# A graph network on one core: the SBUF map of two stages redrawn

## The reference

```python
# L0: sparse weight matrix built from the edges
x = _layernorm(x + (x @ W.T + bias))
# L1: RMS norm, 1024 -> 256, graph attention with 4 heads (softmax over the incoming edges), 256 -> 1024
x = _layernorm(x + _L1(x, edge_index, rms_w, W_down, Wl, Wr, att, W_up))
# L2: graph convolution
x = _layernorm(x + relu(segment_sum((x @ W)[src] * norm, dst) + b))
# L3: two graph layers of the form  h @ W_self + mean(h[src]) @ W_neigh + b
x = _layernorm(x + _L3(x, src, dst, W_self0, W_neigh0, b0, W_self1, W_neigh1, b1))
```

## Time and profile before

| | us |
|---|---|
| median of three runs | 1559.93 |
| the profiled execution, first to last instruction | 1553.5 |
| TensorE busy | 1433.6 (92%) |
| VectorE busy | 783.6 (50%) |
| ScalarE busy | 421.9 (27%) |
| GpSimd busy | 254.4 (16%) |

### The profile page before, as it was taken

The page is one execution under the profiler, slowest core; times in us unless marked ns, Lnnn a source line. Parts: engine busy times, 40 slices in busy tenths (PEclk is TensorE's granted clock), DMA queues, the critical chain, the costliest instruction groups (busy, mean ns, idle before and its releaser), DMA issues.

```text
span 1553.5 us, 17781 instructions
## 1 busy us (share of the span) xinstructions
PE 1433.6 (92%) x6845; PEld 1145.2 (74%) x6845; DVE 783.6 (50%) x1359; ACT 421.9 (27%) x716; POOL 254.4 (16%) x309
## 2 busy tenths in 40 slices
PE   3988999748999989899999999999999999999996
PEld 3876888625666656678888888888888888888884
DVE  6996776517888868754336632221033232411243
ACT  7853222235565545312111100110120001201000
POOL 3000000064666655110000010000000100000000
PEclk9997999969999999999999999999999999999998
DMA  1665344454555644152117552230056544400252
GB/s 46 192 181 189 106 126 116 93 157 150 163 155 153 179 146 130 55 185 85 61 42 240 180 189 85 103 145 1 0 190 219 187 124 147 143 1 0 91 194 95
DMA packets 101988, 195.95 MB, mean 126 GB/s; under 512 B 26856, under 2 KB 61465, under 8 KB 101905
## 3 DMA queue, kind: packets, MB, share of 16 engines
q1 hardware_dynamic: 77434, 121.01, 25.8%
q0 software_dynamic: 22800, 73.61, 13.9%
q10 hardware_dynamic: 1670, 0.21, 0.1%
HBM read 140.86 MB, written 53.92 MB: 125 GB/s over the span
## 4 chain that ended last, share of the span: by engine, by line
PE 56%; DVE 1%; DMA 0%; issue 0%; POOL 0%; DVEq 0%; ACT 0%
PE layers_y_ps L1927 35%; PE layers_y_ps L1948 17%; PE layers_turn_ps L1911 2%; PE layers_up_ps L1894 1%; PE layers_y_ps L1964 1%; DMA x_d<-fetched_x 0%; DVE layers_w_lo L2082 0%; DVE layers_y L2126 0%; PE layers_y_ps L1972 0%; DVE layers_y L597 0%; DVE layers_ln_stats L591 0%; PE layers_turn_ps L1882 0%; DVE layers_parts_lo L2099 0%; DVEq L592 0%; PE layers_y_ps L1882 0%
## 5 line engine op out<-in xcount | busy, mean ns | idle before, releaser
L1948 PE MATMUL layers_y_ps<-layers_parts_hi,layers_counts 128*128 128x512 f32 x464 | 143.6, 391 | 0.0
L1948 PE MATMUL layers_y_ps<-layers_parts_lo,layers_counts 128*128 128x512 f32 x464 | 143.3, 390 | 0.0
L1927 PE MATMUL layers_y_ps<-layers_w_hi,layers_parts_hi 128*128 128x512 f32 x400 | 126.0, 396 | 0.0
L1927 PE MATMUL layers_y_ps<-layers_w_lo,layers_parts_hi 128*128 128x512 f32 x400 | 123.6, 390 | 0.0
L1927 PE MATMUL layers_y_ps<-layers_w_hi,layers_parts_lo 128*128 128x512 f32 x400 | 123.5, 390 | 0.0
L509 POOL DMA_INDIRECT attention_got<-xl_d,attention_src x104 | 106.5, 1024 | 63.1 <-DVE attention_weighted L1537 31.3
L1948 PEld LDWEIGHTS layers_y_ps<-layers_parts_lo,layers_counts 128*128 128x128 f32 x464 | 87.1, 188 | 18.7
L1948 PEld LDWEIGHTS layers_y_ps<-layers_parts_hi,layers_counts 128*128 128x128 f32 x464 | 86.9, 188 | 18.9
L1353 PE MATMUL attention_mix_ps<-attention_weighted,attention_hot 128*110 128x260 f32 x368 | 95.7, 384 | 3.7 <-DVE attention_weighted L1537 3.7
L1320 PE MATMUL attention_row_ps<-attention_bent,edges_att_rows 128*128 128x512 f32 x184 | 97.1, 611 | 0.0
L2099 DVE SCALAR_TENSOR_TENSOR layers_parts_lo<-layers_y_ps,layers_parts_hi 128x1024 fp32r<-128x1024 f32 x16 | 19.6, 1225 | 147.5 <-ACT layers_parts_hi L2043 147.5
(11 more groups left out here) (341 smaller groups left out, 2783.4 us busy)
## 6 DMA issues: line engine op xcount, KB each, us to landing
layers_counts<-counts_d SPq DMA_DIRECT2D x30, 640.0 KB, 4.0
layers_rest<-x_d SPq DMA_DIRECT2D x23, 512.0 KB, 4.1
self_d<-layers_y POOLq DMA_DIRECT2D x20, 512.0 KB, 6.0
x_d<-layers_y POOLq DMA_DIRECT2D x19, 512.0 KB, 2.9
fetched_x<-x_d SPq DMA_DIRECT2D x17, 512.0 KB, 3.7
fetched_raw<-in_L_gnn_W_self POOLq DMA_DIRECT2D x16, 512.0 KB, 5.9
fetched_raw<-in_L_gnn_W_neigh POOLq DMA_DIRECT2D x16, 512.0 KB, 9.0
heads_dst_wide<-in_dst_held SPq DMA_DIRECT2D x13, 512.0 KB, 4.0
```

The lines of the kernel that those rows point to most:

```text
L1927: last = nc.tensor.matmul(y_ps[n % 2][:, a:a + HALF], rows_in[t][:, k * P:(k + 1) * P], w[k][:, a:a + HALF], start=(k == 0 and p == 0), st ...
L1948: last = nc.tensor.matmul(y_ps[n % 2][:, a:a + HALF], counts[c % 2][:, k, :], part[k][:, a:a + HALF], start=(k == 0 and part is hi), stop= ...
```

## The change

No instruction is added, removed or moved. Only addresses change.

- `Memory.at` places a tile at a given address. The 10 tiles of weights and `up` parts of `Fetched` now lie at `base`, which is where the tiles held through the attention end (57.5 KiB). A tile named `split_weights` keeps that room free of other tiles in both stages.
- In attention the tiles from `xr` on are allocated behind that room, in a new order: `xr`, `hot_t`, `bent`, `score_rows`, then the small index tiles, `scaled`, `got`, `dst_wide1`, `far`, and the rest as before.
- In the layers `w_hi3` and `w_hi4` lie in front of the room, and behind it `parts_lo`, `counts`, `w_hi5` to `w_hi7`, `w_lo3` to `w_lo7`, `y`, `side`, `rest`, `mixed_hi` and `mixed_lo`.
- `raw`, `x` and `mixed` of `Fetched` move up to the top of SBUF.

The addresses, in KiB, as they follow from the allocations:

| tile | before | after |
|---|---|---|
| all_ident | 16.1 to 16.6 | the same |
| layers parts_hi | 17.4 to 49.4 | the same |
| layers parts_lo | 49.4 to 81.4 | 97.5 to 129.5 |
| layers w_hi3, w_hi4 | 81.4 to 89.4 | 49.4 to 57.4 |
| layers w_hi5 to w_hi7 | 89.4 to 101.4 | 139.5 to 151.5 |
| layers w_lo3 to w_lo7 | 101.4 to 121.4 | 151.5 to 171.5 (4 each) |
| layers y | 121.4 to 129.4 | 171.5 to 179.5 |
| layers counts | 137.4 to 147.4 | 129.5 to 139.5 |
| layers mixed_hi, mixed_lo | 147.4 to 151.4 | 187.5 to 191.5 |
| fetched x1, x0 | 156.0 to 160.0, 160.0 to 164.0 | 196.0 to 200.0, 200.0 to 204.0 |
| fetched raw | 164.0 to 184.0 | 204.0 to 224.0 |
| fetched up_lo, up_hi | 184.0 to 200.0 | 81.5 to 97.5 |
| fetched w_lo, w_hi (k = 0 to 2) | 200.0 to 224.0 | 57.5 to 81.5 |
| attention xr | 61.7 to 64.7 | 97.5 to 100.5 |
| attention got (6 of 7) | 64.7 to 88.7 | 124.7 to 148.7 |
| attention hot_t | 88.7 to 100.7 | 100.5 to 112.5 |
| attention bent, score_rows | 104.7 to 110.7, 122.7 to 124.7 | 112.5 to 120.5 |
| attention shift, shifted_rows | 124.9 to 128.0 | 164.9 to 168.0 |
| attention hot, weighted | 128.2 to 148.3 | 168.2 to 188.3 |
| front stage: xt_hi, dense w_lo, dense w_hi | 113.6 to 121.6, 160.0 to 192.0, 192.0 to 224.0 | the same |

The diff, cut to its core:

```diff
+SPLIT_TILES = 2 * (3 + KH)
+    def at(self, name, shape, offset, dtype=F32):
+        return self.nc.alloc_sbuf_tensor_at(f"{self.stage}_{name}", shape, dtype, offset=offset)
 # attention_stage
+        xr = slots("xr", [P, HID], F32R, 3)
+        hot_t = slots("hot_t", [P, WINDOW], F32R, 3)
+        bent = slots("bent", [P, HALF], F32, 3)
+        score_rows = m.sb("score_rows", [P, HALF], F32R)
         src = [first_src] + slots("src", [P, SUB_TILES], I32)
         dst = slots("dst", [P, SUB_TILES], I32, 4)
+        scaled = slots("scaled", [P, HALF])
+        got = [first_got] + slots("got", [P, QUAD, HID], F32, GOT - 1)
         wide = [dst_wide, m.sb("dst_wide1", [P, WINDOW], I32)]
...
 # class Fetched
-        self.w_hi = [m.sb(f"w_hi{k}", [P, FEAT], F32R, side="right") for k in range(3)]
...
+        def held(name, place):
+            return m.at(name, [P, FEAT], base + place * FEAT * 4, F32R)
+        self.w_hi = [held(f"w_hi{k}", k) for k in range(3)]
+        self.w_lo = [held(f"w_lo{k}", 3 + k) for k in range(3)]
+        self.up_hi = [held(f"up_hi{k}", 6 + k) for k in range(KH)]
+        self.up_lo = [held(f"up_lo{k}", 6 + KH + k) for k in range(KH)]
 # layers_stage
         parts_hi = m.sb("parts_hi", [P, BLOCKS - KH, FEAT], F32R)
+        below = (fetched.base - nc.sbuf_base) // (FEAT * 4)
+        own_hi = [m.sb(f"w_hi{SPLIT + k}", [P, FEAT], F32R) for k in range(below)]
+        m.sb("split_weights", [P, SPLIT_TILES * FEAT + (fetched.base - nc.sbuf_base) // 4])
         parts_lo = m.sb("parts_lo", [P, BLOCKS - KH, FEAT], F32R)
+        counts = [m.sb(f"counts{s}", [P, BLOCKS, P], F32R) for s in range(2)]
+        own_hi += [m.sb(f"w_hi{k}", [P, FEAT], F32R) for k in range(SPLIT + below, KB)]
...
-        counts = [m.sb(f"counts{s}", [P, BLOCKS, P], F32R) for s in range(2)]
 # graph_layers
+                m = Memory(nc, inner, "fenced")
+                base = nc.sbuf_base
+                m.sb("split_weights", [P, SPLIT_TILES, FEAT])
+                fetched = Fetched(Memory(nc, ctx, "fetched"), io, base)
```

More of the change, by code:

```diff
@@ L1122, in slots @@
             return [m.sb(f"{name}{s}", shape, dtype) for s in range(n)]
+        xr = slots("xr", [P, HID], F32R, 3)
+        hot_t = slots("hot_t", [P, WINDOW], F32R, 3)
+        bent = slots("bent", [P, HALF], F32, 3)
+        score_rows = m.sb("score_rows", [P, HALF], F32R)
         src = [first_src] + slots("src", [P, SUB_TILES], I32)
         dst = slots("dst", [P, SUB_TILES], I32, 4)
+        scaled = slots("scaled", [P, HALF])
+        got = [first_got] + slots("got", [P, QUAD, HID], F32, GOT - 1)
         wide = [dst_wide, m.sb("dst_wide1", [P, WINDOW], I32)]
[L1127 to L1131, removed]
         far = slots("far", [P, WINDOW], F32, 3)
-        score_rows = m.sb("score_rows", [P, HALF], F32R)
         unit_max = slots("unit_max", [P, QUADS, KH])
@@ L1631, with __init__ @@
 class Fetched:
-    def __init__(self, m, io):
-        self.w_hi = [m.sb(f"w_hi{k}", [P, FEAT], F32R, side="right") for k in range(3)]
-        self.w_lo = [m.sb(f"w_lo{k}", [P, FEAT], F32R, side="right") for k in range(3)]
-        self.up_hi = [m.sb(f"up_hi{k}", [P, FEAT], F32R, side="right") for k in range(KH)]
-        self.up_lo = [m.sb(f"up_lo{k}", [P, FEAT], F32R, side="right") for k in range(KH)]
+    def __init__(self, m, io, base):
+        def held(name, place):
+            return m.at(name, [P, FEAT], base + place * FEAT * 4, F32R)
+        self.base = base
+        self.w_hi = [held(f"w_hi{k}", k) for k in range(3)]
+        self.w_lo = [held(f"w_lo{k}", 3 + k) for k in range(3)]
+        self.up_hi = [held(f"up_hi{k}", 6 + k) for k in range(KH)]
+        self.up_lo = [held(f"up_lo{k}", 6 + KH + k) for k in range(KH)]
         self.raw = [m.sb(f"raw{r}", [P, FEAT], side="right") for r in range(KB - 3)]
@@ L1690, in layers_stage @@
         parts_hi = m.sb("parts_hi", [P, BLOCKS - KH, FEAT], F32R)
+        below = (fetched.base - nc.sbuf_base) // (FEAT * 4)
+        own_hi = [m.sb(f"w_hi{SPLIT + k}", [P, FEAT], F32R) for k in range(below)]
+        m.sb("split_weights", [P, SPLIT_TILES * FEAT + (fetched.base - nc.sbuf_base) // 4])
         parts_lo = m.sb("parts_lo", [P, BLOCKS - KH, FEAT], F32R)
+        counts = [m.sb(f"counts{s}", [P, BLOCKS, P], F32R) for s in range(2)]
+        own_hi += [m.sb(f"w_hi{k}", [P, FEAT], F32R) for k in range(SPLIT + below, KB)]
         hi = [parts_hi[:, t, :] for t in range(BLOCKS - KH)] + [t[:, :] for t in fetched.up_hi]
         lo = [parts_lo[:, t, :] for t in range(BLOCKS - KH)] + [t[:, :] for t in fetched.up_lo]
-        w_hi = [t[:, :] for t in fetched.w_hi + [m.sb(f"w_hi{k}", [P, FEAT], F32R) for k in range(SPLIT, KB)]]
+        w_hi = [t[:, :] for t in fetched.w_hi + own_hi]
         w_lo = [t[:, :] for t in fetched.w_lo + [m.sb(f"w_lo{k}", [P, FEAT], F32R) for k in range(SPLIT, KB)]]
@@ L2312, in graph_layers @@
                 dense.close()
-                fetched = Fetched(Memory(nc, ctx, "fetched"), io)
+                m = Memory(nc, inner, "fenced")
+                base = nc.sbuf_base
+                m.sb("split_weights", [P, SPLIT_TILES, FEAT])
+                fetched = Fetched(Memory(nc, ctx, "fetched"), io, base)
                 attention_stage(nc, g, io["src_held"], io["dst_held"], xl_d, xr_d, best, summed, x1_d, mixed_d, fetched,
```

## The result

The changed kernel is slower. Its median is 1563.64 us (1557.07 to 1570.58, 20 runs), against 1559.28 us (1551.43 to 1564.54, 20 runs) for the kernel before beside it. The ratio is 1.0035, with a 95% interval of 1.0019 to 1.0052, so +3 to +8 us. The forecast was 1556.4 us, 3.5 less than before, with a range up to 1562. The time lies above the range and the sign is wrong.

The account below looks back on a forecast made before the run. TensorE's matmul steps were taken to bound the kernel. Sums -2.8, dense units -2.4, turns +0.4 and attention +1.3 gave -3.5 us, so 1556.4 us against 1559.9, with a range of 1549 to 1562.

Parts of the forecast that it names:

- What bounds the kernel: Whole kernel, mainly the layers: TensorE, busy 92% of the span; a ns off a matmul's step comes off the end.
- What the step depends on: Layers' matmuls: one operand in a low region and the other in a high one (a crossing) costs about 6.7 ns.
- Where the border lies: SBUF: low and high regions meet at 160 KiB, for moving (inferred) and stationary operands alike.
- Sums: Layers' 30 sum units: all operands become low, so crossings and tails worth 92 ns a unit go, -2.8 us.
- Dense units: Layers' 50 dense units: crossings remain only for w_lo5 to w_lo7, 173 to 124 ns a unit, -2.4 us.
- tail: Layers: after crossings end, the next 8 matmuls stay slightly slow, about 37 ns in all.
- Turns: Layers' transposes of x and y with the identity: x and y go above the border and leave tails, +0.4 us.
- Attention: Attention: products of shift and transposes of shifted_rows become crossings, +1.3 us, between nothing and 2.6, wider end 8.3.
- The other engines: VectorE and others: the tiles' new places cost nothing, and in the layers TensorE hides their work.
- The slower one: Layers and attention: moving border at 128 KiB, dense units +2.6 us, sum up to +8.5 us, 1568.4 us; 8%.
- rivals 2 to 4: No tail after two crossings, 1551.4 us, 14%; border above 171.5 KiB, 1549.4, 9%; border at 128 KiB, 1568.4, 8%.
- Rival 1: Whole kernel: an operand's place isn't the cause of the slow steps, so the time stays, 0, 1559.9 us; 6%.

Follow-up runs that it names:

- e1: Kernel before, with an unused 32-byte tile at the top of SBUF, so all tiles placed from the top lie 32 bytes lower: 1543.89 us against 1552.55, ratio 0.9937.
- e8: As e1, with the two counts tiles alone 32 bytes higher: 1549.39 us against 1552.66 for the kernel before, ratio 0.9979.
- e5: Changed kernel, with only parts_hi, w_hi3 and w_hi4 96 bytes higher in the layers: 1546.17 us against 1553.84 for the kernel before, ratio 0.9938.
- e7: As e1, with the front stage's xt_hi and its kind moved from offset 64 to 192: 1544.21 us against 1553.84 for the kernel before, ratio 0.9921.
- e9: As e1, with parts_lo alone 32 bytes higher: 1552.91 us in one run.
- e2: Changed kernel, with an unused 32-byte tile ahead of base, so tiles at offset 32 come to 64: 1556.75 us, 1.0028 of the kernel before.
- e4: As e1, with the layers' own w_hi and w_lo from k = 3 up 64 bytes further, counts0 128, counts1 256: 1547.36 us in one run.
- e6: As e1, with the layers' weights from k = 3 up 96 bytes further, counts0 288, counts1 128 modulo 256: 1560.3 us in one run.
- e3: Kernel before, with an unused 96-byte tile at the top of SBUF, so tiles placed from the top lie 96 bytes lower: 1545.68 us in one run.

## Why the prediction was wrong

**What bounds the kernel: right.** All that moved the time in these runs moved it through TensorE's steps in the layers and the front stage. In the layers, what a row of the chain gained or lost came out at the end. Adding up what each step takes beyond 226.67 ns (its excess) over all 8 phases gives 11.3 us for the kernel before, 18.3 for the changed one and 0.5 for e1. The layers of the profiles (from their first matmul to their last) took 886.5, 893.8 and 875.4 us, so +7.3 and -11.1 where the steps say +7.0 and -10.9.

**What the step depends on: the step that failed.** That an address has a price was right, and so were its size, 6.7 ns, and the refusal of the rule by which a place is worth nothing. The Trainium skill, "SBUF — State Buffer" (Who interferes with whom), says that PE's two read ports are independent and that PE never waits on anyone, which leaves no room for such a difference; e1 and e8 show 226.7 and 233.3 ns for the same instructions, so the measurement decides. Wrong was what of the address counts. The forecast compared regions and distances in KiB, and saw correctly that neither "high" nor "far" fitted. It then took the one grouping left, low by high, without asking in what else the two groups differed. The top of SBUF gave offset 224 and the bottom 192. The addresses in whole KiB hid that. In the rows it rests on, each pair called a crossing has offsets that differ by 32 and each other pair has none.

**Where the border lies: no run shows one.** In e1 and e5 all steps of the layers are at 226.7 ns, with tiles on either side of 160 KiB, and the border's two supports fall with e1 and e7. The front stage was slow for offsets of 64 and 224, not for `w_lo` beginning at 160 KiB. The turns of `x0` and `x1` differed by 0.03 us. In e1 both tiles lie where they lay, on the two sides of the supposed border, and both units take 10.90 us. After the change the seven such units in a row take 11.15 each, in both phases that turn `x`. What made the 0.03 us isn't known, but it was no measure of a border, and too thin a row to carry the map.

**Sums, -2.8 us forecast, +3.6 measured.** The excess of the 30 units went from 2.9 to 6.4 us. `up` by `counts` lost its price as foretold. But `parts_hi` by `counts` now differs by 160, 16 of 40 matmuls, and the 16 with `parts_lo` between them pay as neighbours: e9 shows that such neighbours do.

**Dense units, -2.4 us forecast, +3.4 measured.** The excess went from 8.5 to 11.8 us. In a unit of blocks 0 to 7 the two passes by `parts_hi` differ by 96 (but for `w_hi3` and `w_hi4`), and by `parts_lo` only those two do, by 160. The rest pays as neighbours, so all 48 matmuls do, where 18 and a tail did before. Blocks 8 and 9 stand at 229.6 ns on average, a little below the 231.2 of before, when 30 of their 48 matmuls differed. e5 takes both terms away at once with three tiles moved by 96 bytes, which settles the two sizes as one cause.

**Turns, +0.4 us.** Not seen: in e5, with `x` above 196 KiB, the units with a turn take 10.90 or 10.91 us, as in e1.

**Attention, +1.3 us forecast: open.** In the eleven profiles its length comes in two groups, 326 to 329 and 332 to 334 us, with both maps in either. In the long one the old map has 332.0, 332.5, 332.8 and 332.9 and the new one 333.7 and 334.2, +1.4 us. The rows of its products don't back that up: `shift` products take 476 ns on average in the changed kernel and 447 and 451 in e2 and e5, with 446 to 461 for the old map. The transposes of `shifted_rows` take 274 ns against 273. If there is an effect, it is not the one that was argued.

**The other engines: right.** VectorE's subtraction takes 1219 ns in its new place, against 1219 and 1220.

**The rivals.** The slower one reached the right sign and nearly the size in the dense phases (127.7 or more was its mark, 127.8 came). It was wrong all the same, since it left the sums fast. Its mark shared a flaw with the forecast: rivals 2 to 4 took the grouping of the addresses for granted and varied only where it ends and what a tail costs. Rival 1 held that the place isn't the cause, and e1 and e8 refute it. Of +7.0 us in steps and up to 1.4 in the attention, the medians show 4.4 (3 to 8).

## What to carry to other kernels

Give the moving and the stationary tiles of a dense run of 512-column float32r matmuls starts that are equal modulo 256 bytes, also from one matmul to the next, and check it after every change of the map, since one odd tile of 32 bytes shifts all that are placed behind it. It is worth 0.6 to 0.8% here, for a line or two that compute nothing. And before an address effect is put down to regions, write the addresses in bytes and look for everything in which the fast and the slow pairs differ; a tile of 32 bytes that nobody uses is the cheapest experiment there is.

## What the runs showed of the hardware

The step of a matmul of 512 float32r columns, each with its own weight load, by the difference of the two starts modulo 256. These are means over stretches of one difference, from the starts of single matmuls in the traces (granted clock about 1.00, the level of 2.4 GHz):

| difference | step, ns | seen in |
|---|---|---|
| 0 (and 256) | 226.7 | e1, e5, e7; e4 with `counts1` 227.3 with a tail |
| 32 | 233 | before; e6 with `counts0` |
| 64 | 229 | e3, e4; front stage of e3, 230.7 |
| 96 | 234 | e6 |
| 128 | 232 to 233 | e4 and e6, sums; front stage of e1 |
| 160 | 234 | front stage before, |
| 192 | 233 | e3 |
| 224 | 233 | e8; before, |

**Which two tiles meet.** Where the difference changes, the starts of single matmuls show more than the table. After twelve or more matmuls whose tiles agree, a change of the moving tile makes the step slow that starts at the first matmul to read it: 226.7 ns ahead of it, 235.0 there, at 199 places. A change of the stationary tile makes the step ahead of that matmul slow already, 233.6 ns at 23 places (the changed kernel, e2, e4, e8, e9), though the matmul that runs in it has two tiles that agree. And at five places in the kernel before, from block 7 to block 8 of a dense phase, no matmul has tiles that differ: both stand at 192 up to the last of block 7, and both at 224 from the first of block 8. The timeline of the kernel before, then that of e1, where all stand at 192:

```profile
780.11 0.62 PE L1927 MATMUL layers_y_ps<-layers_w_hi,layers_parts_lo 128*128 128x512 f32 x2
780.57 0.62 PE L1927 MATMUL layers_y_ps<-fetched_w_hi,fetched_up_hi 128*128 128x512 f32 x2
...
782.41 0.62 PE L1927 MATMUL layers_y_ps<-fetched_w_lo,fetched_up_hi 128*128 128x512 f32 x2
```

```profile
778.58 0.62 PE L1927 MATMUL layers_y_ps<-layers_w_hi,layers_parts_lo 128*128 128x512 f32 x2
...
780.85 0.62 PE L1927 MATMUL layers_y_ps<-fetched_w_lo,fetched_up_hi 128*128 128x512 f32 x2
```

Ten steps take 2.30 us before and 2.27 in e1. Single steps show that the last one of block 7 takes 235 ns and the seven behind it 230, 224, 231, 236, 228, 233 and 231, then 226.7 again: about 35 ns in all for one meeting of a moving tile at 192 with the next matmul's stationary tile at 224. (In e3 the same five meetings differ by 64, and there the slow steps begin one later: 226, 229, 233 and 231.) The weight load of that next matmul starts 3 ns after the current matmul in the traces and takes 188. So by these places what has to agree is the moving tile of a matmul and the stationary tile that is loaded beside it. In a long stretch of one pair of tiles the two readings are the same, which is why the table and the runs above don't tell them apart. The seven steps behind a single meeting are also why aligned matmuls between others pay, and 35 ns is the size of the forecast's tail.

**What stays open.** Why the two starts have to agree, and why a difference of 64 costs 2.7 ns where 192 costs 6.6, was not tried. Nor is it known why the slow steps go on behind such a meeting and sometimes don't: `up` in the changed kernel is at 226 ns from its first step. All of this was seen at one width and one type, and it may not hold at another: the front stage's 230 products of 256 columns into `down` have tiles that agree and step at 120.0 ns in the kernel before, while those into `xl` and `xr`, with a difference of 192, step at 117.4. No run moved only these.
